# A three-layer graph network with a gated update and routed experts on one core: unit columns reordered, node rows by transfer and VectorE transpose, the update written as z*h + (1-z)*n

## The reference

```python
A = (adj != 0)
for i in range(3):                      # graph stage
    m = einsum('bnd,de->bne', h, weight[i])
    aggr = einsum('bst,bsd->btd', A, m)
    gi, gh = aggr @ w_ih.T + b_ih, h @ w_hh.T + b_hh
    r = sigmoid(i_r + h_r);  z = sigmoid(i_z + h_z)
    n = tanh(i_n + r * h_n)
    h = (1.0 - z) * n + z * h
x = x + h
H = gelu(layernorm(x) @ W1 + b1)        # then softmax(H @ Wg + bg), its argmax e,
x = x + prob[e] * (H @ Wd[e] + bd[e])   # and that expert
```

## Time and profile before

| | |
|---|---|
| time, median of 3 runs | 491.79 us (491.76 to 492.24) |
| span of the profiled execution, first to last instruction | 490.1 us |
| busy: PE, PE weight loads, DVE, ACT, POOL | 480.0, 401.9, 370.0, 334.7, 376.1 us |

### The profile page before, as it was taken

The page is one execution under the profiler, slowest core; times in us unless marked ns, Lnnn a source line. Parts: engine busy times, 40 slices in busy tenths (PEclk is TensorE's granted clock), DMA queues, the critical chain, the costliest instruction groups (busy, mean ns, idle before and its releaser), DMA issues.

```text
span 490.1 us, 10428 instructions
## 1 busy us (share of the span) xinstructions
PE 480.0 (98%) x3247; PEld 401.9 (82%) x3247; DVE 370.0 (76%) x1158; ACT 334.7 (68%) x595; POOL 376.1 (77%) x371
## 2 busy tenths in 40 slices
PE   8999999999999999999999999999999999999994
PEld 4788888888888888888888877777769999999994
DVE  4898678789887898888887798878977555655552
ACT  4886996667976768966787698988763554445531
POOL 5389986789988899979778656777777776377576
PEclk9999999999999999999999999999999999999998
DMA  8889000000000000000000000111353342233110
GB/s 217 234 242 289 0 1 0 1 1 1 1 1 2 0 1 2 0 3 0 1 0 1 0 2 18 59 62 57 110 136 100 119 124 86 71 97 90 33 48 24
DMA packets 37317, 27.38 MB, mean 56 GB/s; under 512 B 6140, under 2 KB 33920, under 8 KB 37264
## 3 DMA queue, kind: packets, MB, share of 16 engines
q1 hardware_dynamic: 31344, 17.40, 12.8%
q0 software_dynamic: 4320, 8.93, 5.2%
q10 hardware_dynamic: 1600, 0.40, 0.4%
HBM read 17.12 MB, written 10.04 MB: 55 GB/s over the span
## 4 chain that ended last, share of the span: by engine, by line
PE 94%; ACT 2%; DVE 2%; POOL 1%; issue 1%; POOLq 0%; DVEq 0%
PE bank L484 20%; PE bank L486 19%; PE bank L485 19%; PE bank L736 13%; PE bank L507 4%; PE bank L531 4%; PE bank L530 4%; PE bank L672 3%; PE bank L722 2%; PE bank L629 1%; PE bank L596 1%; PE bank L537 1%; ACT adj_i L948 1%; PE bank L564 1%; PE bank L569 0%
## 5 line engine op out<-in xcount | busy, mean ns | idle before, releaser
L948 ACT ACTIVATE adj_i<-bank,b1c 128x512 f32<-128x512 f32 (+1 forms) x136 | 91.3, 685 | 72.8 <-PE bank L486 72.3
L375 POOL TENSOR_TENSOR diff<-hT,n_sb 128x512 f32<-128x512 f32 x48 | 77.1, 1607 | 12.0 <-ACT n_sb L834 12.0
L451 POOL DMA_INDIRECT sorted_rows<-xrow,pos x64 | 62.2, 972 | 20.0 <-issue 17.9
L736 PE MATMUL bank<-wd_sb,adj_i 128*128 x568 | 66.7, 275 | 0.0
L377 POOL TENSOR_TENSOR diff<-z_sb,diff 128x512 f32<-128x512 f32 x48 | 63.5, 1323 | 3.8
L736 PEld LDWEIGHTS bank<-wd_sb,adj_i 128*128 128x128 f32 x568 | 65.1, 192 | 0.2
L484 PE MATMUL bank<-ag_hi,wf_hi 128*128 128x512 f32 x144 | 61.0, 424 | 0.0
L484 PE MATMUL bank<-hT_hi,w_hi 128*128 128x512 f32 (+1 forms) x136 | 58.3, 429 | 0.9 <-ACT adj_i L948 0.7
L486 PE MATMUL bank<-ag_hi,wf_lo 128*128 128x512 f32 x144 | 57.1, 397 | 0.0
L485 PE MATMUL bank<-ag_lo,wf_hi 128*128 128x512 f32 x144 | 56.7, 394 | 0.0
L484 PE MATMUL bank<-hT_hi,whh_hi 128*128 128x512 f32 x132 | 54.0, 409 | 0.0
(11 more groups left out here) (185 smaller groups left out, 1158.2 us busy)
## 6 DMA issues: line engine op xcount, KB each, us to landing
adj_i<-sorted_rows SPq DMA_DIRECT2D x71, 72.0 KB
xrow<-in_x_dram SPq DMA_DIRECT2D x16, 256.0 KB, 3.7
adj_i<-in_adj_dram SPq DMA_DIRECT2D x16, 256.0 KB, 4.0
sorted_rows<-xrow,pos POOLq DMA_INDIRECT x64, 2.3
sorted_rows<-padrow SPq DMA_DIRECT2D x9, 72.0 KB
out_dram<-cand,home POOLq DMA_INDIRECT x39
bd_bc<-in_L_ffn_bd_dram SPq DMA_DIRECT2D x1, 512.0 KB, 4.1
out_dram<-n_sb,home POOLq DMA_INDIRECT x32
```

Source lines behind the costliest of these rows:

```text
L375: nc.gpsimd.tensor_tensor(diff[:, b, :], hT[:, g, :], n_sb[:, b, :], ALU.subtract).then_inc(diff_ok, 1)
L451: nc.gpsimd.indirect_dma_start(out=sorted_rows, out_offset=bass.IndirectOffsetOnAxis(ap=pos[:, g, j:j + 1], axis=0), in_=xrow[:, g * GR + ...
L736: last = nc.tensor.matmul(o, HT[:, sg % 2, k, j * P:(j + 1) * P], wd_sb[:, bass.ds(at + k * P, P)], start=(k == 0), stop=(k == KC - 1))
L948: nc.scalar.activation(HT[:, hb, k, 0:n], HB[k][:, 0:n], ACT.Gelu, bias=b1c[:, k:k + 1]).then_inc(done, 1)
```

## The change

- The columns of a unit are no longer ordered graph by graph. They stand as strip (a quarter of a graph, 32 nodes), graph, token of the strip: column = strip x 128 + graph x 32 + token. TensorE writes its transposes and neighbour sums in that order (`by_graph`), as four pieces of 32 columns per graph.
- The node rows of a new state no longer come from TensorE. SP issues four SBUF-to-SBUF transfers after each state (`state_banded`), VectorE transposes 32x32 blocks (`state_rows`) three steps after the unit. hn and A are fp32, and one fp32 product per graph takes the place of the two on hn_hi and hn_lo.
- The residual moves from VectorE to GpSimd.
- The update is z*h (`old_part`) and (1-z)*n (`new_part`), both on GpSimd; ScalarE makes 1-z as a second sigmoid (`keep`); VectorE's sum `state(s - 1)` stands in step s, where `state(s - 2)` stood before, and stands now ahead of `reset(s)`.
- Half of the x and adj transfers and all expert weights are issued between units' transfers. Row statistics of the last group and GpSimd's last scales come one gate step later.

```diff
+        def by_graph(o):
+            return o.rearrange("p (s g e) -> p g s e", s=QP, g=GR)
...
+            def state_banded(u):
+                b = u % 2
+                sp.wait_ge(h_ok, u + 1)
+                hold(sp, hn_ok, u - 1)
+                for q in range(QP):
+                    sp.dma_start(bands[q * SUB:(q + 1) * SUB, b, :],
+                                 hT[:, u % QUAD, q * P:(q + 1) * P]).then_inc(band_in[b], 16)
...
+            for u in range(UN):
+                state_banded(u)
+                if inside(u - QUAD, GROUPS - FIRST_LOADS):
+                    load_group(u - QUAD + FIRST_LOADS)
+                k = u - (2 * UNITS - QUAD)
...
+                if k == 1:
+                    sp.dma_start(wd_sb[:].rearrange("p (e k c) -> p e k c", e=E, k=KC),
...
-            def old_state(u):
-                g, b = u % QUAD, u % 2
+            def old_part(u):
+                b = u % 2
+                hold(pool, z_ok, made("all", u))
+                hold(pool, h_ok, made("all", u - 2))
+                nc.gpsimd.tensor_tensor(diff[:, b, :], z_sb[:, b, :], hT[:, u % QUAD, :], ALU.mult).then_inc(zh_ok, 1)
+            def new_part(u):
+                b = u % 2
                 hold(pool, n_ok, made("all", u))
-                nc.gpsimd.tensor_tensor(diff[:, b, :], hT[:, g, :], n_sb[:, b, :], ALU.subtract).then_inc(diff_ok, 1)
-                hold(pool, diff_ok, made("all", u))
-                nc.gpsimd.tensor_tensor(diff[:, b, :], z_sb[:, g, :], diff[:, b, :], ALU.mult).then_inc(zd_ok, 1)
+                hold(pool, kept_ok, made("all", u))
+                nc.gpsimd.tensor_tensor(n_sb[:, b, :], n_sb[:, b, :], keep[:, b, :], ALU.mult).then_inc(nk_ok, 1)
+            def residual(u):
+                hold(pool, hn_ok, u + 1)
+                gx = xres[:, graph0(u):graph0(u) + GR, :].rearrange("p g (i j) -> p g i j", j=QP)
+                nc.gpsimd.tensor_tensor(gx, gx, hn[:, u % 2, :].rearrange("p (g j i) -> p g i j", g=GR, j=QP),
+                                        ALU.add).then_inc(x1_ok, 1)
...
             def step_gnn(s):            # GpSimd
-                if first(s + 1):
-                    first_rows_low(s + 1)
                 if exists(s - 1):
-                    old_state(s - 1)
+                    new_part(s - 1)
...
+                if exists(s):
+                    old_part(s)
+                u = s - 3
+                if exists(u) and layer(u) == LAYERS - 1:
+                    residual(u)
...
-                    nc.tensor.matmul(pAG[:, c], hn_hi[:, u % 2, c], A[:, u % QUAD, c], start=True, stop=False)
-                    last = nc.tensor.matmul(pAG[:, c], hn_lo[:, u % 2, c], A[:, u % QUAD, c], start=False, stop=True)
+                    last = nc.tensor.matmul(by_graph(pAG[:])[:, j], rows_of[:, c],
+                                            A[:, u % QUAD, c].rearrange("p (s e) -> p s e", s=QP), start=True, stop=True)
...
-                    for j in range(GR):
-                        last = nc.tensor.transpose(pF[:, j * P:(j + 1) * P], hT[:, u % QUAD, j * P:(j + 1) * P], ident[:])
...
+                nc.scalar.activation(keep[:, u % 2, :], pZ[:], ACT.Sigmoid, bias=bkeep[:, 0:1], scale=-1.0).then_inc(kept_ok, 1)
...
+            def state_rows(u):          # VectorE
+                b = u % 2
+                dve.wait_ge(band_in[b], banded(u))
+                if u >= 2:
+                    hold(dve, ag_ps, made("all", u + QUAD - 2) if layer(u - 2) < LAYERS - 1 else 0)
+                    hold(dve, x1_ok, made("last", u - 2))
+                nc.vector.transpose(hn[:, b, :].rearrange("p (g j e) -> p j g e", g=GR, j=QP),
+                                    bands[:, b, :].rearrange("p (j g e) -> p j g e", g=GR, j=QP)).then_inc(hn_ok, 1)
...
             def step_gnn(s):            # VectorE
-                if exists(s - 2):
-                    state(s - 2)
-                if exists(s - 3) and layer(s - 3) == LAYERS - 1:
-                    residual(s - 3)
+                if exists(s - 3):
+                    state_rows(s - 3)
...
+                if exists(s - 1):
+                    state(s - 1)
                 if exists(s):
                     reset(s)
                     candidate(s)
```

192 lines of the change are left out of this document (78 added, 114 removed).

## The result

The changed kernel takes 521.96 us (median of 4 runs, 521.24 to 523.32); the kernel before took 491.93 on the same chip. The ratio is 1.061 (95% interval 1.0598 to 1.0623). The forecast was 502.2 with a range of 489 to 513: slower, as forecast, but by three times as much. In the table of experiments, runs marked * were made while their chip ran the kernel before in 558 to 563 us, with the same steps in the graph stage (steps 4 to 11 of e2, e3, e5 and e13, where nothing was edited, agree with e4's to 0.04 us), so of those runs only A(0) to A(47) and the first gate groups are read, and their ratios don't compare with the others.

A forecast was written before the change was run, and what follows sets the result against it. TensorE was taken as the bound (94% of the chain of waits); -21.1 + 9.9 + 7.5 + 4.8 + 2.0 + 2.0 + 4.8 + 0.5 = +10.4 on 491.8 gave 502.2 us, range 489 to 513.

The forecast's parts named there:

- transposes gone: TensorE: row transposes of layers 1 and 2 and of the last layer's output go, 48 groups at 0.44 us: -21.1 us.
- row-scale steps, laps of GpSimd: Steps 4 to 7, 16 to 19, 28 to 31: GpSimd's laps of 6.08 us exceed the limit: +9.9 us.
- steps 14, 26, 38: residual ahead of new: GpSimd's low half, old product and residual precede the new product, which ends 2.5 us past its limit: +7.5 us.
- steps 24, 36: gate's scales: GpSimd: scales of sixteen graphs, 4.03 us, delay the new product 2.4 us past its limit in two steps: +4.8 us.
- other low-half steps: Steps 40 to 45 and one or so per cycle: two-step loop gives 5.27 us a step against 5.09: +2.0 us.
- opening: First steps: keep adds ScalarE work to three steps and unit 1's sum waits for tanh and GpSimd's product: +2.0 us.
- hand-over and the gate's first groups: Hand-over to the gate: VectorE's sum of unit 47 stands ahead of the gate's second low half: +4.8 us.
- last scales behind stores: GpSimd's last scales move behind its first four stores, so other stores come 4.0 us later: +0.5 us.
- Rival (c): Split PSUM writes by neighbour products and transposes are slow: about 540 to 550 us; chance 0.03.
- (a): Graph stage: TensorE stays the bound and GpSimd's lateness is absorbed: 473 to 478 us; chance 0.14.
- (b): In between: stalls of steps 14, 26, 38 and the scales half as long, laps 5.85: 488 to 492 us; chance 0.10.
- (d): Transfers land late and VectorE's transposes wait ahead of the state sum: 510 to 530 us; chance 0.07.

The follow-up runs named there:

- e2: Changed kernel with extra unread TensorE products filling five graph-stage stops; step 0 to step 47 took 282.2 us, ratio 1.043 to the kernel before.
- e3: Changed kernel with GpSimd's residual ahead of the low half and old product; step 0 to step 47 took 274.3 us, ratio 1.032 to the kernel before.
- e5: Changed kernel with the gate's first two batches of scales moved to steps 34 and 46; step 0 to step 47 took 279.1 us, ratio 1.035.
- e13: Changed kernel with the residual on VectorE instead of GpSimd; step 0 to step 47 took 277.2 us, ratio 1.037 to the kernel before.
- e4: Changed kernel run again, unedited; 519.9 us, ratio 1.056 to the kernel before.
- e9: Changed kernel with GpSimd held behind its new product until VectorE's sum is done, in five steps; 516.2 us, ratio 1.050 to the kernel before.
- e12: Changed kernel with extra unread TensorE products filling five graph-stage stops and the one at the gate's start; 515.1 us, ratio 1.048.
- e18: e10 with row scale back ahead, state_rows ahead of the sum in steps 8 and 9 of each cycle, last unit's rows later; 484.04 us, ratio 0.984.
- e10: e7 with expert weights in eight transfers, constants behind candidate, row scale behind old_part, gate's low halves ahead of statistics; 490.7 us, ratio 0.997.
- e6: Changed kernel with VectorE's sum back two steps later, state_rows behind it and the row statistics; 493.1 us, ratio 1.002 to the kernel before.
- e8: Kernel before with only the update's operations and the sum's new place, row transposes left on TensorE; 512.7 us, ratio 1.042.
- e11: Changed kernel with VectorE's last sum, state(47), in step 49 instead of 48; 519.7 us, ratio 1.056 to the kernel before.
- e17: Changed kernel with ScalarE's last tanh ahead of the gate's first two gelus; gate's first four groups took 23.9 us, ratio 1.047.
- e1: Changed kernel with VectorE's sum behind reset and candidate; step 0 to step 47 took 280.6 us, ratio 1.042 to the kernel before.
- e7: e6 with GpSimd's residual also put ahead of the low half and old product; 491.7 us, ratio 0.999 to the kernel before.

## Why the prediction was wrong

By its own steps, each measured from the step lengths over 5.09 or 5.53:

| step of the sum | forecast | measured |
|---|---|---|
| transposes gone | -21.1 | -21.1 (steps of 5.09, 5.53) |
| row-scale steps, laps of GpSimd | +9.9 | +8.8 |
| steps 14, 26, 38: residual ahead of new | +7.5 | +15.5 (5.95, 5.33, 4.2) |
| steps 24, 36: gate's scales | +4.8 | +10.6 (5.0, 5.6) |
| other low-half steps | +2.0 | +4.1 |
| opening | +2.0 | +1.7 (A(3) comes 1.3 later, with one group of transposes gone) |
| hand-over and the gate's first groups | +4.8 | +8.5 (0.3 + 6.9, and 1.3 for three groups of transposes gone) |
| last scales behind stores | +0.5 | +1.3 (the time lost there; its cause was not tested) |
| sum | +10.4 | +29.4 of 30.0 |

What held: TensorE's steps, laps of 6.0 (GpSimd's new products begin at 117.10, 123.15, 129.13 and 135.11 in the profile after), the steps with the long stops, TensorE's busy share in the graph stage (92%), neighbour products of eight passes, hidden transfers and VectorE transposes (0.70 each). The releaser held in part: ag_lo ended 22 waits of 10.4 us in all, but the five longest stops, 12.1 us together, stand ahead of the third group of products with the old state and were ended by VectorE's reset (L1134), which waits behind the sum just the same. Rival (c) falls by the 0.81 us above, and by the first layer's transposes, the same instructions as before, still 0.44 a group (5.53 - 5.09): with pieces of 128 bytes no run shows the slowing that the prediction kept as a rival. Rivals (a) and (b) fall with the stops; (d) needed 8 us for the transfers, and VectorE waited 0.4 for them in all. The time lies in (d)'s range, but not by (d)'s mechanism. The working has small slips: the new product ends at 3.48 + 3.80 = 7.28 and not 7.35, the scales' term is (4.7 - 2.4) x 2 = 4.6 and not 4.8, the loop of two steps 5.25 a step and not 5.27. They move the forecast by less than 1 us.

**The step that failed** is the price of a stop: "Counted back: 5.09 - 0.69 (ag_lo) - 0.61 (candidate) - 0.86 (reset) - 0.60 (the sum, as a VectorE operation of 512 columns) = 2.33". How late GpSimd is was right (A + 4.02 for 4.0, and A + 5.33 for 4.7 behind the scales, of which 0.5 is the residual's 1.78 for 1.25). How much that costs was not, for two reasons, each shown by a run:

- The sum reads both inputs from SBUF and lasts 1.67, not 0.60, where a GpSimd operation of 512 columns began just before it. In the profile after the 48 sums take 40.4 us where 48 x 0.68 is 32.6, and the five stops have it each time. Two more stand elsewhere: the last unit's, and that of unit 9 (1.71), which is why step 11 took 6.85 where steps 23 and 35, with sums of 0.69, took 5.90 and 5.88. It was in sight: before, the sums averaged 0.89 us, harmless two steps ahead of need. Undisturbed in five places (e9): 5.4 less in the graph stage, part of it the clock's.
- After stops TensorE's clock was at 1.2 GHz, half, for 3.4 to 6.8 us each time: 44 products 0.19 us longer. Filled (e12): 5.7 less in the graph stage, 1.3 in the gate. The prediction put the clock at nothing.

The graph stage lost 15 us beyond the forecast (39.0 for 24.2). Added up, the two runs give 11 of them, but they overlap, and no run has both edits. In e4's graph stage 40 products of 512 columns began at the lower clock and in e9's 20; at 0.195 us each up to 3.9 of e9's 5.4 are the clock's. So the two reasons are worth 7 to 11 us together, an estimate from these counts. Another 1 is the residual's length ahead of the scales, another 1 the long sum in step 11 (read from the trace, no run takes it apart), and the rest, 2 to 6, stays open.

The hand-over's term had the right place and only part of the cause. The sum began at 309.67, where the chain puts it, but took 1.92, and the clock fell behind the stop; these are the same two reasons. Yet moving the sum gained nothing, the tanh 0.9 to 1.6, the residual 0.6 to 1.3, the clock 1.3, where two profiles of the changed kernel differ by 0.7. Even e18 needs 19.4 us for the four groups where before has 18.6. No single edit carries that loss. That it is the whole later chain (last product, four transfers, turn, residual, statistics, and the stops that come one behind another) is what fits, argued and not shown; e10 to e18, which move several of these at once, bring most of it back.

## What to carry to other kernels

An operation that moves one step closer to its use takes its whole queue with it: what counts is what stands behind it on its engine, and two steps of cushion for one were worth 27 us here (e6). Whether z*h + (1-z)*n costs anything by itself no run shows, since none has it alone with the old cushion. A wait's price is not only its length; look in the trace of before for how an operation's length varies (mean against shortest) and who was busy beside it, and add what the clock does after a stop. When two reasons lengthen the same stop, two runs that each remove one don't add up. When a second engine is late, try first what can be done while it idles (the residual ahead of the low half), then the order on the engine that waits.

## What the runs showed of the hardware

- VectorE's sum with two SBUF inputs takes 0.69 us alone and 1.66 to 1.92 when a GpSimd operation of 512 columns began just before it. Where the sum began first (unit 21, 147.23 against 147.32) it kept 0.69, and GpSimd's operation took 1.76 in place of 1.27. VectorE's operations that read PSUM keep 0.65 to 0.74 beside the same operations (76 of them in the profile after). The Trainium skill ("SBUF — State Buffer", SBUF: two separate sides) says that the two engines share a port pair, held exclusively by whichever starts first. The trace agrees: GpSimd's operation began at 105.03, the sum at 105.17, and it ended 0.56 after GpSimd's.
- TensorE's clock fell to half behind stops of 1.8 to 5.7 us; behind e9's stop of 1.3 us at 108.8 and in all of e8's graph stage, with none above 1.1, it stayed at full. Nor did it fall behind each long one: the stop at 107.6 cost it in four profiles (after, e4, e11, e17) and not in e5's, and e1 kept the full clock (1.00 from 165 to 240) behind its stop of 2.87 us at 171.1.
- Writing PSUM in four pieces of 32 columns costs nothing: eight passes in 0.81 against 0.84 before, four transposes 0.44 as before.
- Four 64 KB transfers within SBUF land in 2.2 us each (median) and are hidden in the changed kernel's order (VectorE waits 0.4 us for them in all); behind a 2 MB transfer one unit's were late enough to make VectorE wait 2.93 us (e7).
- A residual with a strided operand takes GpSimd 1.52 to 1.60 us, against 1.27 for its plain products, and 1.77 to 1.99 where VectorE's adjacency conversion or sum was under way as it began.
